# Feed-forward stage of a four-stage block: quantised values turned by transposing transfers instead of on TensorE, with the down product a tile later

## What is computed

```python
def _act_quant(x):
    scale = 127.0 / jnp.clip(jnp.max(jnp.abs(x), axis=-1, keepdims=True), 1e-05)
    xq = jnp.clip(jnp.round(x * scale), -128.0, 127.0) / scale
    return x + jax.lax.stop_gradient(xq - x)
def _weight_quant(w):
    scale = 1.0 / jnp.clip(jnp.mean(jnp.abs(w)), 1e-05)
    wq = jnp.clip(jnp.round(w * scale), -1.0, 1.0) / scale
    return w + jax.lax.stop_gradient(wq - w)
def _bitlinear(x, w):
    return jnp.einsum('bsd,fd->bsf', _act_quant(x), _weight_quant(w))
h = jax.nn.silu(_bitlinear(x, W1))      # W1: 2048 x 512
return _bitlinear(h, W2)                # W2: 512 x 2048
...
x = x + _L0_ffn_ref(_layernorm(x, axis=-1), L0_ffn_W1, L0_ffn_W2)
```

## Time and profile before

| | us |
|---|---|
| Median of 3 runs (lowest to highest) | 1141.57 (1141.57 to 1142.78) |
| The profiled execution | 1142.28 |
| Its span in the profile | 1140.4 |
| TensorE busy in the span | 987.2 (87%) |
| VectorE busy | 766.9 (67%) |
| ACT busy | 652.9 (57%) |
| POOL busy | 264.7 (23%) |

### The profile page before, as it was taken

How to read it: one execution, slowest core, us unless ns; L and a number is a source line. 1 busy time by engine, 2 the same in 40 slices (tenths; PEclk the granted TensorE clock), 3 DMA queues, 4 the chain that set the end, 5 groups by cost and what they waited for, 6 DMA issues and landing times. The chain is left out here.

```text
span 1140.4 us, 20554 instructions
## 1 busy us (share of the span) xinstructions
PE 987.2 (87%) x7516; PEld 776.8 (68%) x7516; DVE 766.9 (67%) x1656; ACT 652.9 (57%) x1687; POOL 264.7 (23%) x224
## 2 busy tenths in 40 slices
PE   0789999997308999876899999899999999999587
PEld 0678888886203555443788888788887888888475
DVE  5466776665576999625676767567675767777466
ACT  2477777766366888644554555445554555455275
POOL 0555556434013433011001010010101001000381
PEclk9999999999758999998999999999999999999798
DMA  6400000000409100051000000000000000000012
GB/s 244 162 7 6 7 6 7 1 2 2 148 22 299 30 1 1 1 204 38 20 1 20 1 20 2 3 20 1 20 1 4 18 1 1 1 1 2 0 38 112
DMA packets 19816, 41.92 MB, mean 37 GB/s; under 512 B 1024, under 2 KB 4352, under 8 KB 19200
## 3 DMA queue, kind: packets, MB, share of 16 engines
q1 hardware_dynamic: 17072, 32.14, 8.7%
q10 hardware_dynamic: 2640, 8.39, 1.9%
HBM read 36.33 MB, written 4.19 MB: 36 GB/s over the span
## 5 line engine op out<-in xcount | busy, mean ns | idle before, releaser
L1304 ACT ACTIVATE c_h<-c_bank_b 128x512 fp32r<-128x512 f32 x64 | 38.2, 597 | 155.5 <-PE c_bank_b L1236 155.5
L526 POOL TENSOR_TENSOR a_probs<-a_probs,a_inv 128x256 f32<-128x256 f32 (+1 forms) x128 | 102.6, 827 | 106.1 <-DVE a_inv L584 106.1
L1318 ACT ACTIVATE probs<-c_score,c_neg_max 128x256 f32<-128x256 f32 x256 | 119.1, 480 | 13.6 <-DVE c_neg_max L1379 13.6
L1092 POOL TENSOR_TENSOR c_ctx_raw<-c_ctx_raw,c_table 128x1024 f32<-128x1024 f32 x8 | 19.1, 2381 | 450.8 <-PE c_bank_b L1236 365.9
L434 ACT ACTIVATE a_probs<-a_s,a_neg_max 128x128 f32<-128x128 f32 (+1 forms) x256 | 104.0, 433 | 26.6 <-DVE a_neg_max L572 26.0
L1369 DVE TENSOR_TENSOR c_l<-c_bank_b,c_h 128x512 fp32r<-128x512 f32 x64 | 44.3, 691 | 100.9 <-ACT c_h L1304 100.9
L1309 ACT ACTIVATE c_pT_h<-c_turn 128x512 fp32r<-128x512 f32 x128 | 69.9, 596 | 60.7 <-PE c_turn L1226 60.7
L44 PE MATMUL c_acc<-VO_h,c_l 128*128 128x512 f32 x256 | 100.8, 394 | 1.9 <-DVE c_l L1369 1.9
L46 PE MATMUL c_acc<-VO_h,c_h 128*128 128x512 f32 x256 | 100.5, 392 | 0.0
L45 PE MATMUL c_acc<-VO_l,c_h 128*128 128x512 f32 x256 | 100.0, 391 | 0.0
L1379 DVE TENSOR_REDUCE c_neg_max<-c_score 128x2 f32<-128x512 f32 x128 | 82.0, 682 | 7.1 <-PE c_score L1215 7.1
(11 more groups left out here) (252 smaller groups left out, 2837.2 us busy)
## 6 DMA issues: line engine op xcount, KB each, us to landing
g_x<-in_x ACTq DMA_DIRECT2D x4, 1024.0 KB, 15.7
w_raw<-in_w ACTq DMA_DIRECT2D x1, 4096.0 KB, 14.3
w_raw<-in_w SPq DMA_DIRECT2D x4, 1024.0 KB, 9.2
wq<-in_wq SPq DMA_DIRECT2D x1, 4096.0 KB, 24.0
c_ctx_raw<-in_ctx SPq DMA_DIRECT2D x8, 512.0 KB, 3.6
wo<-in_wo SPq DMA_DIRECT2D x1, 4096.0 KB, 14.2
out<-g_x SPq DMA_DIRECT2D x16, 256.0 KB, 2.1
aw_raw<-in_wq SPq DMA_DIRECT2D x1, 1024.0 KB, 7.5
```

Of the source, the lines that this page charges most:

```text
L526: last = pool.tensor_tensor(p, p, inv[:, pair, q, :].unsqueeze(2).broadcast_to([P, 2, (q + 1) * P]), ALU.mult)
L1318: last = act.activation(probs[p % 2][:, i, :], score[h][:, t, :], ACT.Exp, bias=neg_max[:, i:i + 1], accum_out=sums[:, i:i + 1])
```

## The change

The transposes on TensorE and the copies on ACT are gone, with their PSUM tensors xT and hT and their semaphores. In their place SP issues, for each 128x128 chunk, a transfer from SBUF to SBUF with `transpose=True`: 4 a tile from xq to xqT, 16 a tile from hq to hqT. xqT, hq, hqT and down have two buffers each, s2 has three columns. The down product of tile t-1 stands in step t, behind up of t+2, and the addition and the statistics of tile t-2 in step t on VectorE. The loop has two more steps. The four loads for the third stage are issued by ACT, ahead of its first step.

```diff
--- before.py
+++ after.py
@@ -770,27 +770,25 @@
 
         y, yr = [m.sb(f"y{i}", [P, D]) for i in range(2)], m.sb("yr", [P, D])
         xq = [m.sb(f"xq{i}", [P, D], BF16) for i in range(2)]
-        xqT = m.sb("xqT", [P, DC, P], BF16)
-        s1, s2 = m.sb("s1", [P, 2]), m.sb("s2", [P, 2])
+        xqT = [m.sb(f"xqT{i}", [P, DC, P], BF16) for i in range(2)]
+        s1, s2 = m.sb("s1", [P, 2]), m.sb("s2", [P, 3])
         h = [m.sb(f"h{i}", [P, F]) for i in range(2)]
-        hr, hq = m.sb("hr", [P, F]), m.sb("hq", [P, F], BF16)
-        hqT = m.sb("hqT", [P, FC, P], BF16)
+        hr, hq = m.sb("hr", [P, F]), [m.sb(f"hq{i}", [P, F], BF16) for i in range(2)]
+        hqT = [m.sb(f"hqT{i}", [P, FC, P], BF16) for i in range(2)]
         amax, unit, q_scale = m.sb("amax", [P, 2]), m.sb("unit", [P, 2]), m.sb("q_scale", [P, 2])
         stats = m.sb("stats", [P, 6])
         up = m.ps("up", [P, F])
-        xT = m.ps("xT", [P, DC, P], BF16)
-        hT = m.ps("hT", [P, FC, P], BF16)
-        down = m.ps("down", [P, D])
-        y_ready, x_quant, x_turned, x_copied = m.sem("y_ready"), m.sem("x_quant"), m.sem("x_turned"), m.sem("x_copied")
+        down = [m.ps(f"down{i}", [P, D]) for i in range(2)]
+        y_ready, x_quant, x_turned = m.sem("y_ready"), m.sem("x_quant"), [m.sem(f"x_turned{i}") for i in range(2)]
         upped, silued = m.sem("upped"), m.sem("silued")
         h_scaled, h_rounded, h_quant = m.sem("h_scaled"), m.sem("h_rounded"), m.sem("h_quant")
-        h_turned, h_copied, downed, added = m.sem("h_turned"), m.sem("h_copied"), m.sem("downed"), m.sem("added")
-        HALF = FC // 2
+        h_turned, downed, added = [m.sem(f"h_turned{i}") for i in range(2)], m.sem("downed"), m.sem("added")
+        X_TURN, H_TURN = DC * DMA, FC * DMA
 
         def all_steps(eng, step):
 
 
-            for t in range(-3, TILES):
+            for t in range(-3, TILES + 2):
                 step(t, t % 2)
 
         def has(t, ahead):
@@ -806,56 +804,49 @@
             @block.sync
             def _(sp):
 
-                wq, kcq, wqr, kckv = ahead
-                sp.dma_start(kcq, io["kcq"].rearrange("h (c p) k -> p h c k", p=P)).then_inc(ahead_in, DMA)
-                sp.dma_start(wqr, io["wqr"].rearrange("h (c p) r -> p h c r", p=P)).then_inc(ahead_in, DMA)
-                sp.dma_start(wq, io["wq1"].rearrange("(h k) d -> k h d", k=P)).then_inc(ahead_in, DMA)
-                sp.dma_start(kckv, io["kckv"].rearrange("h k d -> k h d")).then_inc(ahead_in, DMA)
+                def turn_tokens(t):
+                    sp.wait_ge(x_quant, t + 1)
+                    after(sp, upped, 2 * (t - 1))
+                    for c in range(DC):
+                        sp.dma_start(xqT[t % 2][:, c, :], xq[t % 2][:, c * P:(c + 1) * P], transpose=True).then_inc(x_turned[t % 2], DMA)
+
+                def turn_hidden(t):
+                    sp.wait_ge(h_quant, t + 1)
+                    after(sp, downed, t - 1)
+                    for c in range(FC):
+                        sp.dma_start(hqT[t % 2][:, c, :], hq[t % 2][:, c * P:(c + 1) * P], transpose=True).then_inc(h_turned[t % 2], DMA)
+
+                def step(t, par):
+                    if has(t, 3):
+                        turn_tokens(t + 3)
+                    if has(t, 1):
+                        turn_hidden(t + 1)
+                all_steps(sp, step)
 
             @block.tensor
             def _(pe):
                 def step(t, par):
-                    if has(t, 0):
-                        pe.wait_ge(h_quant, t + 1)
-                        after(pe, h_copied, 2 * t)
-                        for c in range(FC):
-                            last = pe.transpose(hT[:, c, :], hq[:, c * P:(c + 1) * P], identb[:, :])
-                            if c == HALF - 1:
-                                last.then_inc(h_turned, 1)
-                        last.then_inc(h_turned, 1)
                     if has(t, 2):
-                        pe.wait_ge(x_copied, t + 3)
+                        pe.wait_ge(x_turned[par], ((t + 2) // 2 + 1) * X_TURN)
                         for n in range(4):
                             if n % 2 == 0:
                                 after(pe, silued, 2 * t + 3 + n // 2)
                             for c in range(DC):
-                                last = pe.matmul(up[:, n * D:(n + 1) * D], xqT[:, c, :], w1[:, c, n * D:(n + 1) * D],
+                                last = pe.matmul(up[:, n * D:(n + 1) * D], xqT[par][:, c, :], w1[:, c, n * D:(n + 1) * D],
                                                  start=c == 0, stop=c == DC - 1)
                             if n % 2:
                                 last.then_inc(upped, 1)
-                    if has(t, 0):
-                        after(pe, added, t)
+                    if has(t, -1):
+                        pe.wait_ge(h_turned[1 - par], ((t - 1) // 2 + 1) * H_TURN)
+                        after(pe, added, t - 2)
                         for c in range(FC):
-                            if c % HALF == 0:
-                                pe.wait_ge(h_copied, 2 * t + 1 + c // HALF)
-                            last = pe.matmul(down[:, :], hqT[:, c, :], w2[:, c, :], start=c == 0, stop=c == FC - 1)
+                            last = pe.matmul(down[1 - par][:, :], hqT[1 - par][:, c, :], w2[:, c, :], start=c == 0, stop=c == FC - 1)
                         last.then_inc(downed, 1)
-                    if has(t, 3):
-                        pe.wait_ge(x_quant, t + 4)
-                        after(pe, x_copied, t + 3)
-                        for c in range(DC):
-                            last = pe.transpose(xT[:, c, :], xq[1 - par][:, c * P:(c + 1) * P], identb[:, :])
-                        last.then_inc(x_turned, 1)
                 all_steps(pe, step)
 
             @block.scalar
             def _(act):
                 def step(t, par):
-                    if has(t, 0):
-                        for i in range(2):
-                            act.wait_ge(h_turned, 2 * t + i + 1)
-                            act.activation(hqT[:, i * HALF:(i + 1) * HALF, :], hT[:, i * HALF:(i + 1) * HALF, :], ACT.Copy
-                                           ).then_inc(h_copied, 1)
                     if has(t, 1):
                         act.wait_ge(h_scaled, t + 2)
                         after(act, h_quant, t + 1)
@@ -867,9 +858,12 @@
                             cols = slice(n * F // 2, (n + 1) * F // 2)
                             act.activation(h[par][:, cols], up[:, cols], ACT.Silu, scale=s1[:, par:par + 1]
                                            ).then_inc(silued, 1)
-                    if has(t, 3):
-                        act.wait_ge(x_turned, t + 4)
-                        act.activation(xqT[:], xT[:], ACT.Copy).then_inc(x_copied, 1)
+
+                wq, kcq, wqr, kckv = ahead
+                act.dma_start(kcq, io["kcq"].rearrange("h (c p) k -> p h c k", p=P)).then_inc(ahead_in, DMA)
+                act.dma_start(wqr, io["wqr"].rearrange("h (c p) r -> p h c r", p=P)).then_inc(ahead_in, DMA)
+                act.dma_start(wq, io["wq1"].rearrange("(h k) d -> k h d", k=P)).then_inc(ahead_in, DMA)
+                act.dma_start(kckv, io["kckv"].rearrange("h k d -> k h d")).then_inc(ahead_in, DMA)
                 all_steps(act, step)
 
             @block.gpsimd
@@ -891,17 +885,17 @@
                 def add_output(t, par):
                     dve.wait_ge(downed, t + 1)
                     xt = X[:, t, :]
-                    dve.scalar_tensor_tensor(xt, down[:, :], s2[:, par:par + 1], xt, ALU.mult, ALU.add
+                    dve.scalar_tensor_tensor(xt, down[par][:, :], s2[:, t % 3:t % 3 + 1], xt, ALU.mult, ALU.add
                                              ).then_inc(added, 1)
 
                 def scale_hidden(t, par):
                     dve.wait_ge(silued, 2 * t + 2)
                     dve.tensor_reduce(amax[:, 1:2], h[par][:, :], AX.X, ALU.max, apply_absolute_value=True)
                     scales(1).then_inc(h_scaled, 1)
-                    dve.tensor_scalar(s2[:, par:par + 1], unit[:, 1:2], mean[:, 1:2], None, ALU.mult)
+                    dve.tensor_scalar(s2[:, t % 3:t % 3 + 1], unit[:, 1:2], mean[:, 1:2], None, ALU.mult)
 
                 def quantise_tokens(t, par):
-                    after(dve, x_turned, t - 1)
+                    after(dve, x_turned[t % 2], t // 2 * X_TURN)
                     dve.wait_ge(y_ready, t + 1)
                     dve.tensor_reduce(amax[:, 0:1], y[par][:, :], AX.X, ALU.max, apply_absolute_value=True)
                     scales(0)
@@ -913,15 +907,15 @@
 
                 def quantise_hidden(t):
                     dve.wait_ge(h_rounded, t + 1)
-                    after(dve, h_turned, 2 * t)
-                    dve.tensor_scalar(hq[:, :], hr[:, :], -MAGIC, 127.0, ALU.add, ALU.min).then_inc(h_quant, 1)
+                    after(dve, h_turned[t % 2], t // 2 * H_TURN)
```

(12 more changed lines are left out.)

## The result

The changed kernel takes 1428.49 us (median, 1426.39 to 1433.30), the kernel before 1142.07 in the same runs: a ratio of 1.251, 95% interval [1.248, 1.255], +286.4 us. The forecast was 1405, the range 1185 to 1685.

What follows compares the result with a forecast made beforehand. TensorE was taken to set the 8.02 us step, VectorE 3% behind. With SP's transfers setting the pace afterwards, the stage would end at 371.1 + 369.6 + 9.4 = 750.1 against 486.45, +263.7 us: 1405 us, range 1185 to 1685.

Steps and rivals of the forecast that it cites:

- c, the distance between transfers: Time on SP's queue from one 128x128 transposing transfer to the next: 1.2 us, 308 of them giving 369.6 us.
- Rival 1: On SP, a turning transfer costs about a plain one, 0.33 to 0.9 us: 1157 to 1313 us; chance 0.28.
- Rival 2: On SP, transfers nearly serialise up to their landing, 1.6 us each upwards; at 2.1, 1683 us; chance 0.25.
- Rival 3: Turning transfers pace below 0.35 us and ACT isn't held, so the step shortens to 7.07 us: 1135 us; chance 0.05.
- ACT's hold: At the stage's start, four load issues hold ACT until 361.34; first SiLU at 362.62, its end 13.1 us later.
- tokens 0 to 2 under cover: At the start, turning token tiles 0 to 2 fits within 18 us of cover from the wait for ACT.
- The tail: After SP's last issue: landing 2.1, down to addition 5.3, then next stage 2.0, together 9.4 us.
- Nothing else differs: Outside the feed-forward stage nothing changes; the next stage's loads have long landed.
- The slack of the second buffers: Second buffers and down a tile later let SP's queue run without gaps but can't shorten it; 9.3 us against 24.

Runs made afterwards that it cites:

- the run with pieces: The changed kernel with its 320 transfers, the four loads taken from the head of ACT's queue and issued in 16 pieces behind ACT's steps -1 to 14: 1418.07 us.

## Why the prediction was right, and where not

**c, the distance between transfers: right in kind, small by 7%.** The 308 transfers from the first inner one (375.53) to the end of the last issue (738.89 + 33.11 = 772.00) took 396.5 us, 1.287 each, against 1.2: +26.9 us, the largest term of the miss. (Undisturbed ones follow at 1.27; single issues of up to 2.17 us bring the mean to 1.287.) The middle of two far ends was close by luck; nothing in the trace of before held the number. The argument I gave for a price above a plain issue, that a turned tile is broken up into short pieces, was wrong: 4 chunks in one transfer, or half a chunk, cost the same 1.2 us. The better question would have been whether the price is one of the issue or of the bytes, since it decides what to change. The figure of the Trainium skill (VectorE: DVE Perf Modes, The three transpose paths), 1309 ns for 128x128, is near to the pace of single transfers (1.287), and the trace agrees to 2%. As a price of the turning it would be wrong by much: 16 chunks in one transfer hold the queue for 1.908 us.

**Rival 1** (c as of a plain transfer) fell: 1.232 against 0.332 us. (By the sum's own base its 1157 is 1156.) The statement of the Trainium skill behind it (Advanced Engine Details and Errata, X-Bar Transpose (TRN2)), that transfers that turn are as fast as ordinary ones, doesn't hold for the issue of 32 KB transfers, by the factor 3.7 against the 256 KB stores. No run has an ordinary transfer from SBUF to SBUF. **Rival 2** (serialised up to the landing) fell: they land after 2.3 us and follow at 1.27. **Rival 3** fell with both conditions: 20c = 25.4 us and ACT free at 361.95.

**ACT's hold.** Foreseen to 0.7 us in its place (SiLU at 362.62, measured 363.28). Its price alone was 10.4 us in the changed kernel and not 13.1, since without it the first up isn't as early as in the kernel before: it waits for four issues and a landing, and starts 11.2 us after the stage's beginning in the run with pieces (351.77 - 340.62), against 6.3 before.

**The step that failed: tokens 0 to 2 under cover.** Tile 2 isn't. VectorE quantises its tokens behind the maximum of tile 0, thus behind the late SiLU: xq(2) is written by 370.54 and its four transfers hold SP until 375.5. The first inner transfer goes out at 375.53 and not 371.1: +4.4 us: 0.6 because hq(0) is ready at 371.67 (0.4 of it from the stage's later beginning), and 3.9, rounded, for the tokens of tile 2. I had followed the buffers and semaphores and not VectorE's order.

**The tail**: 9.4 foreseen, 781.34 - 772.00 = 9.3. With 26.9 + 4.4 - 0.1 = 31.2 us the end of the stage, 750.1 foreseen, comes to 781.3.

**"Nothing else differs" was wrong**: later stages gave back 6.9 us. The two errors of the sum had opposite signs, +31.2 and -6.9, and 1405 + 24 = 1429 is within 1 us of the 1428.5 measured.

**The slack of the second buffers**: right that it can't shorten SP's queue. In the single run that separates it, the delay of down by a tile showed no worth in the median; the second buffers were not tried alone.

## What to carry to other kernels

Count the issues on the queue: a transposing transfer from SBUF to SBUF costs its issuer, SP here, some 1.2 us whatever its size up to 128x512, so turn a whole tile in one transfer if at all; 20 a tile were 25 us, 2 a tile 3.1. Even then a transfer in a loop from tile to tile has to be followed through every engine's order, because its landing stands there in series and loads beside it make the landing longer. A load moved to a queue that also computes can hold that engine: the four loads here held ACT until 23.5 us after the stage's beginning.

## What the runs showed of the hardware beyond that

A transfer of 16 chunks of 128x128 turns at 0.12 us a chunk of issue time, and 4.3 us to landing (one chunk alone: 1.232 and 2.3). Landings of turning transfers lengthen beside ordinary loads: 2.3 us alone, 3.5 in the median beside pieces of 0.3 to 1 MB, up to 9.9 beside the whole loads. One load issue on ACT costs 0.37 us when the one before has landed and up to 10.88 behind others. And TensorE has pauses of up to 2.9 us in a late stage, with a lower granted clock behind them, that came with its whole list of instructions in an earlier stage and were gone with every shorter one, 10 us of 1142 in all: a kernel that is changed in one stage can get slower or faster in another, so a gain below 1% is to be read by stage before it is put down to the edit.
